# Softmax reciprocals of a fused attention kernel: from VectorE's reciprocal to a power of minus one on GpSimd

## The chip, the cores and the metric

The kernel runs on one core of a Trainium2 chip. The metric is its time on the device in microseconds, as the median of several executions. Engines: TensorE (PE: matmuls and transposes; PEld is its weight load), VectorE (DVE), ScalarE (ACT), GpSimd (POOL), and SyncE (SP), which issues the DMAs here. TensorE's granted clock was at its upper level (2.4 GHz) in nearly the whole profile, 0.996 of it in the mean.

## The reference

Two layers over x of shape (2, 1024, 256), in float32:

```python
# layer 0
nx = layer_norm(x);  q = nx @ Wq;  k, v = ctx @ Wk, ctx @ Wv        # ctx: (2, 154, 256)
evidence = softmax(q k^T / 16) @ v
combined = concat([nx, evidence, anchor])
probs = softmax(combined @ router_W + router_b)                     # 3 experts
h = silu(combined @ e_w1 + e_b1);  routed = sum_e probs_e * (h_e @ e_w2 + e_b2)
g = sigmoid(silu(combined @ gate_w1 + gate_b1) @ gate_w2 + gate_b2)
x = x + g * (routed @ out_w + out_b)
# layer 1: 16 heads of 16
xq, xkv = ada_ln(x, cond), ada_ln(ctx, cond)
out = concat_heads(softmax(q_h k_h^T / 4) @ v_h)
x = x + out @ Wp + bp
```

The change concerns the softmax of layer 1: the product with v is made with the exponentials as they are, and the result is multiplied by one over their sum.

## The kernel before

The 2048 tokens are worked in eight tiles of 256 (t = 0 to 7; `LAST` is 7, `NEXT` 6). A planner written out by hand (`PLAN`, `PLAN_OF`, `SETUP`) gives each step (a name, a tile and an index) a time slot; `DELAY` shifts it for single engines; and `order(engine)` sorts an engine's steps by that time. So five in-order instruction queues are fixed when the program is built, and semaphores with a name for each step tie them together. While the hidden units of tile t run (seven units; steps `za`, `z`, `h`, `p`: hidden matmuls, tanh on ScalarE, product on VectorE, a split into a high half on ScalarE and a low half `hidden_low` on GpSimd at L1620, second matmul `p`, which reads both halves), the attention of layer 1 of tile t - 1 and t - 2 and the layer 0 attention of tile t + 1 are laid between them.

In layer 1 the steps of a tile are: `stack` (SyncE copies the queries into the stacked layout of head pairs, four groups), `most` (16 score matmuls with the maximum of each taken on VectorE, L1463, in a ring of three banks of PSUM), `row` (the maxima, transposed and copied back), `score` (12 matmuls and exponentials), `value` (matmuls into `value_bank`; its value operand has columns of ones, so that the sums of the exponentials come out as rows of the same result, four rows in each group of 32), `raw` (ScalarE copies the bank to SBUF in two halves, L1142), `sum` on GpSimd, `sums`, `dup`, `out` on VectorE, `out` on ScalarE, `outl` and `proj`.

`sum` adds the four 128x256 slices of the copied result (L1666, L1671, L1673), which leaves in one 128x256 tile the sums of all 16 heads, each in a row of its own. `sums` on VectorE takes the reciprocal in place (L1477):

```python
v.reciprocal(total[:, :], total[:, :]).then_inc(vector_sums, 1)
```

`dup` (L1486) shuffles the outputs so that each stands twice in its group of 32 rows, `out` spreads the reciprocals over the rows with one shuffle for each group (L1496) and multiplies (L1498), ScalarE's `out` rounds the product to its high half, and `outl` (L1506) makes the low half, which `proj` needs. The last tile is worked in two halves with tiles of their own (`last_sums_first`, `last_sums`), and its `sums`, `dup` and `out` come twice.

GpSimd has one in-order queue. In a steady tile its steps around `sum` are: the second pair of adds (L1671, L1673), `probs` of the tile after (two products, L1643 and L1644, whose transposes TensorE does at L1889), `hidden_low` of unit 4 (L1620). It takes rstd of three layer norms as a power of minus one half, in a 128x2 instruction (L1534).

Of the kernel before, what the change touches and what calls it, by code (L numbers as in the profile page):

```python
# [13 lines left out]
ALU = mybir.AluOpType  # L14
# [3 lines left out]
P = 128  # L18
# [71 lines left out]
def packed(np, v):  # L90
# [17 lines left out]
    for b in range(BATCH):  # L108
# [114 lines left out]
        "dup": ["d"],  # L223
        "sums": ["r"],
        "out": ["o"],
# [25 lines left out]
    "tensor": {  # L251
        "norm": 1.4, "qx": 0.31, "prob": 1.4, "keyx": 0.3, "qx_last": 0.2,
    },
    "scalar": {
        "cv": -4.9, "ck": 0.3, "fold": 0.1, "vw": 0.54, "vt": 0.3, "w2": 0.6, "keyx": 0.6, "norm": 1.9, "att": 0.7,
        "logit": 1.7, "z": 0.81, "h": 0.3, "gate": 0.4, "qx": 0.4, "query": 0.1, "row": -0.4, "score": 0.2,
        "out": 1.6, "xhat_last": -0.7, "qx_last": 0.2, "query_last": 0.2, "row_last": 0.5, "score_last": 0,
        "raw_last": 0.1, "out_last": 1.54,
    },
# [3 lines left out]
        "res_last": -1.5, "qn_last": -1.3, "shift_last": -1.1, "qlow_last": 1, "query_last": 1.1, "most_last": 1.5,  # L263
        "row_last": 1.2, "proj_last": -10.8, "dup_last": 0.7, "sums_last": -1.6, "out_last": 1.4, "outl_last": 1.4,
    },
    "gpsimd": {
        "h": 0.6, "ln": 0.86, "qn": -0.2, "low": 0.9, "keyn": 1.2, "split": 2.1,
    },
# [11 lines left out]
PLAN = {  # L280
    "dup": (37.2, 49.2), "za": -0.4, "step": 1.99, "z": 0.38, "h": 1.5, "p": 3.3, "again": -6.4, "vw": -38.8,
    "ln": 0.2, "norm": 1.6, "low": 6.6, "att": 7.9, "prob": 9.1, "route": 12.3, "logit": 14.4, "res": 17.4,
    "qn": 18.4, "shift": 18.5, "xhat": 19.3, "qx": 19.54, "qlow": 20.1, "query": 20.7,
    "most": (22.11, 22.29, 23.89, 24.92, 26.01, 26.34, 27.35, 28.05), "row": (29.2, 30.6),
    "stack": (15.3, 16.8, 20.9, 23.1),
    "score": (32, 32.1, 32.1, 32.7, 33.5, 33.7, 34.2, 34.3, 34.3, 35.4, 35.5, 35.6),
    "value": (33.88, 34.18, 35.92, 36.25), "raw": (35.5, 36.9), "sum": (35.3, 36.4), "sums": (38.1, 47.7),
    "out": (38.34, 56.69), "outl": (43.37, 97.85), "proj": 43.6, "last": (16, 59.3), "reload": 45.3, "init": 5.2,
}

PLAN_OF = {
    0: {
        "most": (21.92, 23.13, 24.17, 24.59, 25.33, 27.11, 27.44, 28.14), "qlow": 19.3, "query": 19.9, "qn": 17.5,
        "h": 1.3, "qx": 18.7, "xhat": 18.2,
    },
    1: {
        "logit": 15.4, "z": 0.62,
    },
# [6 lines left out]
    6: {  # L305
        "init": 6.5, "score": (30.5, 30.6, 30.6, 31.3, 31.4, 31.6, 31.9, 31.9, 31.9, 32.5, 32.6, 33),
        "raw": (34.4, 34.5), "proj": 47.7, "most": (21.9, 22, 24.8, 25.8, 26.5, 27.3, 27.4, 28), "ln": 0.9,
        "value": (31.83, 31.84, 34.15, 34.75), "norm": 1.79, "stack": (16.3, 16.7, 21.5, 21.9),
    },
    7: {  # L310
        "route": 13.2, "most": (19.2, 19.2, 19.3, 19.4, 19.4, 19.6, 20.3, 20.5), "init": 5.6, "sums": (28.4, 36),
        "za": -0.73, "score": (22.06, 22.59, 22.73, 23.07, 23.16, 23.16, 23.63, 23.73, 24.03, 24.23, 24.34, 24.54),
        "outl": (33.4, 33.8), "row": (19.96, 21.53), "h": 1.2, "p": 3.5, "last": (39.5, 39.7), "query": 18.06,
        "xhat": 17.7, "ln": 0.5, "value": (23.2, 23.5, 24.7, 25.8), "proj": 38, "logit": 14.9, "out": (27.3, 33.2),
        "raw": (23.1, 28.7), "qlow": 18, "qx": 17.62, "dup": (24.9, 28.7), "step": 1.96,
    },
}
SETUP = {
    "vw": (1.6, 3, 3.8, 4.5, 6.1, 7.7, 8.2), "vt": (0.8, 2, 2.9, 3.9, 7.1, 9.1, 10.7),
    "unit": (0.99, 2.23, 3.75, 4.08, 9.23, 9.4, 9.94), "w2": (7.4, 10.3, 11.1, 13, 14.2, 17.9), "norm": -0.3,  # L320
    "low": 1.7, "att": 2, "prob": 2.8, "route": 3.8, "logit": 4.75, "cb": 4.3, "bq": 12.2, "split": (8.74, 13.12),
    "keyn": (11.4, 12.5), "keyx": (12.4, 13.8), "key": (13.4, 17.8), "mod": (9.2, 9.6, 10.3, 10.6), "ck": 10.8,
    "fold": (0.6, 12), "late": (6.6, 14.9), "ln": -6.8, "silu": -0, "group": 1.1, "gsplit": 5.6, "setup2": -12,
    "bias1": -7.9,
    "fill": (120.23, 120.27, 120.77, 120.82, 121.09, 121.76, 121.98, 127.05, 127.63, 128.86, 129.54, 129.71, 131.45, 131.47),
    "sel": 114.7, "unstack": 105, "bias2": (26.4, 26.7), "zero": 102.7,
}
# [7 lines left out]
def schedule():  # L335
# [37 lines left out]
    for t in range(NT):  # L373
# [30 lines left out]
        for h in range(parts_of(t)):  # L404
            for name in ("row", "dup", "sums", "out", "outl"):
                place(at + plan(t, name)[h], (name, t, h))
# [40 lines left out]
def build(nc, a, out):  # L447

    with ExitStack() as ctx:
# [199 lines left out]
        def step_sem(engine, stage):  # L649
# [111 lines left out]
        def sums_of(t, h):  # L761
            return (SUMF, SUML)[h] if t == LAST else SUM
# [396 lines left out]
        def _(dve):  # L1159
# [355 lines left out]
            def proj(key):  # L1515
# [6 lines left out]
                     "att": att, "prob": prob, "route": route, "logit": logit, "z": hidden, "init": init, "evac": evac,  # L1522
                     "res": res, "qn": qn, "shift": shift, "qlow": qlow, "query": query, "most": most, "row": row, "dup": dup, "outl": outs_low, "sums": sums,
                     "out": outs, "proj": proj, "last": last_add}
# [5 lines left out]
        def _(pool):  # L1530
# [128 lines left out]
            def sums(key):  # L1659

                t, h = key[1:]
                pool.wait_ge(scalar_raw, upto(scalar_raw, ("raw", t, h), "v"))
                if h == 0:
                    if 0 < t < LAST:
                        pool.wait_ge(vector_out, upto(vector_out, ("out", t - 1, 0), "o"))
                    nc.gpsimd.tensor_tensor(sums_of(t, 0)[:, :], raw_of(t)[:, 0, :], raw_of(t)[:, 1, :], ALU.add).then_inc(gpsimd_sum, 1)  # L1666
                elif t == LAST:
                    nc.gpsimd.tensor_tensor(SUML[:, :], RAWL[:, 2, :], RAWL[:, 3, :], ALU.add).then_inc(gpsimd_sum, 1)
                else:
                    pool.wait_ge(gpsimd_sum, upto(gpsimd_sum, ("sum", t, 0), "s"))  # L1670
# [483 lines left out]
```

## Time and profile before

| | us |
|---|---|
| median of three timed runs | 438.0 (437.63 to 439.25) |
| the profiled execution's own time | 439.08 |
| its span, first to last instruction | 436.9 |
| TensorE busy | 422.1 (97%) |
| VectorE busy | 296.3 (68%) |
| ScalarE busy | 223.6 (51%) |
| GpSimd busy | 175.0 (40%) |
| one steady tile (from a step of one to the same of the next) | 43.3 |

Busy is the time in which an engine has an instruction under way; it says nothing of whether anyone waits for it. Overlapping matmuls are counted once. A time such as "290.60" is microseconds from the span's start. In a timeline the number behind the start is the duration of all instructions merged in the row, whose count stands at the end as x2, x4.

### The profile page before, as it was taken

To read this page: it belongs to the slowest core of one execution; us is meant where nothing else is said; L and a number is where in the kernel's file an instruction comes from. 1 tells how busy PE (TensorE), PEld (TensorE's weight loads), DVE (VectorE), ACT (ScalarE), POOL (GpSimd) and SP (SyncE) were. 2 spreads that over 40 slices of the span, in tenths; PEclk is the share of its full clock that TensorE was granted. 3 is DMA by queue.
4 is the path that set the end of the run, shared out by engine and by line. 5 is a ranking of instruction groups with operands and counts; after the bars stand their busy time and mean duration, and the time that the engine had idled before them with its cause. 6 is when DMAs were issued, how large, how long until landed. Compare 5 with 4: busy or idle time off the path is not lost.

```text
span 436.9 us, 9623 instructions
## 1 busy us (share of the span) xinstructions
PE 422.1 (97%) x3629; PEld 384.7 (88%) x3629; DVE 296.3 (68%) x748; ACT 223.6 (51%) x487; POOL 175.0 (40%) x184
## 2 busy tenths in 40 slices
PE   7899999999999999999999999999999899979996
PEld 6578999989998899889998899889988898868876
DVE  2785566674675696739863797389658755891797
ACT  2868643255347543764367246724672356326271
POOL 4545474553353526324523344344433632330020
PEclk9999999999999999999999999999999999998999
DMA  8786102531100210023000300030003021300301
GB/s 288 252 298 269 50 2 47 142 91 31 44 5 1 63 59 30 24 78 116 2 5 13 109 1 5 14 86 0 5 20 80 0 56 28 80 3 26 72 3 48
DMA packets 16837, 27.80 MB, mean 64 GB/s; under 512 B 3800, under 2 KB 9112, under 8 KB 16664
## 3 DMA queue, kind: packets, MB, share of 16 engines
q1 hardware_dynamic: 16664, 27.19, 21.2%
q8 instruction: 29, 0.48, 0.5%
q14 instruction: 16, 0.13, 0.1%
q10 hardware_dynamic: 128, 0.01, 0.0%
HBM read 15.94 MB, written 2.10 MB: 41 GB/s over the span
## 4 chain that ended last, share of the span: by engine, by line
PE 77%; DVE 15%; issue 3%; ACT 3%; DMA 1%; SPq 1%; ACTq 0%
PE hidden_banks L1688 7%; PE hidden_banks L1690 7%; PE hidden_banks L1689 7%; PE score_banks L1695 6%; PE score_banks L2060 5%; PE token_bank L1688 5%; PE token_bank L1689 5%; PE token_bank L1690 5%; PE score_banks L2030 4%; PE value_bank L2083 3%; PE value_bank L2086 3%; PE value_bank L1695 3%; DVE head_maxima L1463 3%; PE hidden_banks L1913 2%; DVE sums L1477 2%
## 5 line engine op out<-in xcount | busy, mean ns | idle before, releaser
L1620 POOL TENSOR_TENSOR hidden_low<-hidden,hidden_high 128x512 fp32r<-128x512 f32 x56 | 72.8, 1300 | 123.5 <-ACT hidden_high L1072 123.4
L1463 DVE TENSOR_REDUCE head_maxima<-score_banks 128x2 f32<-128x308 f32 x128 | 54.6, 473 | 17.1 <-PE score_banks L2030 15.0
L1688 PE MATMUL hidden_banks<-normed_high,hidden_w_high 128*128 128x256 f32 x224 | 64.2, 287 | 0.8 <-issue 0.8
L1689 PE MATMUL hidden_banks<-normed_high,hidden_w_low 128*128 128x256 f32 x224 | 62.5, 279 | 0.0
L1690 PE MATMUL hidden_banks<-normed_low,hidden_w_high 128*128 128x256 f32 x224 | 62.5, 279 | 0.0
L1132 ACT ACTIVATE exp_ring<-score_banks 128x512 f32<-128x512 f32 x96 | 52.6, 600 | 18.8 <-PE score_banks L2060 17.5
L1072 ACT CAST hidden_high<-hidden 128x512 fp32r<-128x512 f32 x56 | 34.8, 622 | 48.2 <-DVE hidden L1380 48.1
L1688 PE MATMUL token_bank<-expert_out_high,hidden_high 128*128 128x256 f32 x192 | 55.7, 290 | 0.0
L1064 ACT ACTIVATE hidden<-hidden_banks 128x512 f32<-128x512 f32 x56 | 33.3, 595 | 41.6 <-PE hidden_banks L1913 40.0
L1690 PE MATMUL token_bank<-expert_out_low,hidden_high 128*128 128x256 f32 x192 | 53.4, 278 | 0.0
L1689 PE MATMUL token_bank<-expert_out_high,hidden_low 128*128 128x256 f32 x192 | 53.4, 278 | 0.0
L1380 DVE SCALAR_TENSOR_TENSOR hidden<-hidden,hidden_banks 128x512 f32<-128x512 f32 x56 | 38.2, 683 | 18.5 <-ACT hidden L1064 18.3
L1688 PEld LDWEIGHTS hidden_banks<-normed_high,hidden_w_high 128*128 128x128 f32 x224 | 42.1, 188 | 2.1 <-issue 2.0
L1689 PEld LDWEIGHTS hidden_banks<-normed_high,hidden_w_low 128*128 128x128 f32 x224 | 42.3, 189 | 0.1
L1690 PEld LDWEIGHTS hidden_banks<-normed_low,hidden_w_high 128*128 128x128 f32 x224 | 42.0, 188 | 0.0
L1688 PEld LDWEIGHTS token_bank<-expert_out_high,hidden_high 128*128 128x128 f32 x192 | 36.2, 188 | 0.5 <-issue 0.2
L1689 PEld LDWEIGHTS token_bank<-expert_out_high,hidden_low 128*128 128x128 f32 x192 | 36.3, 189 | 0.2
L1690 PEld LDWEIGHTS token_bank<-expert_out_low,hidden_high 128*128 128x128 f32 x192 | 36.1, 188 | 0.0
L2030 PE MATMUL score_banks<-pair_keys,query_stack 96*128 96x308 f32 x112 | 29.4, 335 | 2.5 <-DVE head_maxima L1463 1.4
L1913 PE MATMUL hidden_banks<-probs_T_tail,context_w_tail 100*128 100x256 f32 x112 | 31.6, 282 | 0.0
L1689 PE MATMUL hidden_banks<-probs_T_high,context_w_low 128*128 128x256 f32 x112 | 31.2, 279 | 0.0
L1688 PE MATMUL hidden_banks<-probs_T_high,context_w_high 128*128 128x256 f32 x112 | 31.2, 279 | 0.0
(294 smaller groups left out, 1111.5 us busy)
## 6 DMA issues: line engine op xcount, KB each, us to landing
unit_weights<-units SPq DMA_DIRECT2D x7, 768.0 KB, 6.0
query_stack<-queries_high SPq DMA_DIRECT2D x56, 64.0 KB, 2.0
tokens<-x SPq DMA_DIRECT2D x8, 256.0 KB, 3.7
query_stack<-queries_low SPq DMA_DIRECT2D x28, 64.0 KB, 2.0
w_slice<-units SPq DMA_DIRECT2D x7, 256.0 KB, 3.0
out<-tokens SPq DMA_DIRECT2D x7, 256.0 KB, 2.4
w_T<-folds SPq DMA_DIRECT2D x6, 256.0 KB, 6.1
pair_keys<-keys_high SPq DMA_DIRECT2D x16, 77.0 KB
```

Of the source, the lines that this page charges most:

```text
L1064: nc.scalar.activation(TB[:, ring(t, u), :], Z[:, hidden_bank(t, u), :], ACT.Tanh, scale=0.5).then_inc(scalar_z, 1)
L1072: nc.scalar.copy(SH[:, ring(t, u), :], TB[:, ring(t, u), :]).then_inc(scalar_h, 1)
L1132: nc.scalar.activation(E[:, w % ERING, :], S[:, ring_of[key][0], :], ACT.Exp).then_inc(scalar_score, 1)
L1380: v.scalar_tensor_tensor(out=TB[:, ring(t, u), :], in0=TB[:, ring(t, u), :], scalar=1.0, in1=Z[:, hidden_bank(t, u), :], op0=ALU.add, op1= ...
L1463: v.tensor_reduce(MX[:, s, first:first + step + 1:step], S[:, ring_of[key][0], 0:2 * CTX].rearrange("p (j n) -> p j n", j=2), AX.X, ALU.ma ...
L1620: nc.gpsimd.tensor_tensor(SL[:, ring(t, u), :], TB[:, ring(t, u), :], raw(SH[:, ring(t, u), :]), ALU.subtract).then_inc(gpsimd_h, 1)
L1688: mm(out_, lh, rh, start=start, stop=False, skip_group_check=skip)
L1689: mm(out_, ll, rh, start=False, stop=False, skip_group_check=skip)
L1690: return mm(out_, lh, rl, start=False, stop=stop, skip_group_check=skip)
L1695: last = mm(out_, l, r, start=(i == 0), stop=(i == len(pairs) - 1))
L1913: return mm(half, VWD[0:BROWS, b, c], PTD[0:BROWS, t % 2, :], start=False, stop=True)
L2030: mm(bank, QS[0:STACK, c, P * s:P * s + P], KS[b][0:STACK, c, :, :].rearrange("p j n -> p (j n)"), start=True, stop=True).then_inc(tensor_ ...
```

## The change

The step `sums` is gone from VectorE. GpSimd's `sum` gets a third (or, for the last tile, second) instruction: the power of minus one of the whole 128x256 tile, with an exponent tile of 128x1 broadcast along the row, behind a wait for its own last add. VectorE's `out` waits for GpSimd's `sum` now. The planner's numbers change as well, and with them the order on each engine: on SyncE the store of a finished tile moves ahead of the second group of `stack`, and the reloads of weights in the middle of the kernel (`again`) one place ahead; on VectorE `init` moves behind `qlow`, and in tile 5 `dup` behind `z` of unit 4; on ScalarE `score` 11 moves ahead of the `h` of unit 3 in tiles 2 to 6, and the last tile's `out` of the first half ahead of its second `raw`; on TensorE `prob` of tile 2 moves behind three steps; and a few steps of the setup trade places.

```diff
+        MINUS = put("minus_one", [P, 1])
...
+                v.memset(MINUS[:, :], -1.0)
...
-            def sums(key):
-                t, h = key[1:]
-                total = sums_of(t, h)
-                dve.wait_ge(gpsimd_sum, upto(gpsimd_sum, ("sum", t, 1 if t < LAST else h), "s"))
-                v.reciprocal(total[:, :], total[:, :]).then_inc(vector_sums, 1)
...
             def outs(key):
...
-                dve.wait_ge(vector_sums, upto(vector_sums, key, "r"))
+                dve.wait_ge(gpsimd_sum, upto(gpsimd_sum, ("sum", t, 1 if t < LAST else h), "s"))
...
                 pool.wait_ge(scalar_raw, upto(scalar_raw, ("raw", t, h), "v"))
...
+                total, outs = sums_of(t, h), raw_of(t)
+                add = lambda left, right: nc.gpsimd.tensor_tensor(total[:, :], left, right, ALU.add)
+                if t < LAST and h == 0:
+                    if t:
                         pool.wait_ge(vector_out, upto(vector_out, ("out", t - 1, 0), "o"))
+                    add(outs[:, 0, :], outs[:, 1, :]).then_inc(gpsimd_sum, 1)
+                    return
+                if t == LAST:
+                    add(outs[:, 2 * h, :], outs[:, 2 * h + 1, :]).then_inc(gpsimd_part, 1)
                 else:
                     pool.wait_ge(gpsimd_sum, upto(gpsimd_sum, ("sum", t, 0), "s"))
+                    add(total[:, :], outs[:, 2, :]).then_inc(gpsimd_part, 1)
+                    pool.wait_ge(gpsimd_part, 2 * t + 1)
+                    add(total[:, :], outs[:, 3, :]).then_inc(gpsimd_part, 1)
+                pool.wait_ge(gpsimd_part, 2 * t + 2 if t < LAST else 2 * t + 1 + h)
+
+                nc.gpsimd.tensor_tensor(total[:, :], total[:, :], MINUS[:, :].to_broadcast([P, TILE]), ALU.pow).then_inc(gpsimd_sum, 1)
```

Of the planner's numbers, those that move steps named above:

```diff
-        "row_last": 1.2, "proj_last": -10.8, "dup_last": 0.7, "sums_last": -1.6, "out_last": 1.4, "outl_last": 1.4,
+        "row_last": 1.2, "proj_last": -10.8, "dup_last": 0.7, "sums_last": -1.6, "out_last": 1.4, "outl_last": 1.8,
-        "query": 13.4, "row": -3.6, "proj": 1.5, "last": -2.1, "key": -0.9, "place": 11.3, "query_last": 3.7,
+        "query": 13.4, "row": -3.6, "proj": 1.3, "last": -2.1, "key": -0.9, "place": 11.3, "query_last": 3.7,
-    "stack": (15.3, 16.8, 20.9, 23.1),
+    "stack": (15.5, 17, 21.1, 23.3), "score": (32, 32.1, 32.1, 32.7, 33.5, 33.7, 34.2, 34.3, 34.3, 35.4, 35.5, 35.6),
-    "out": (38.34, 56.69), "outl": (43.37, 97.85), "proj": 43.6, "last": (16, 59.3), "reload": 45.3, "init": 5.2,
+    "out": (38.4, 56.7), "outl": (43.38, 97.79), "proj": 43.7, "last": (16, 59.3), "reload": 45.4, "init": 6.1,
```

## Rows read from the trace of the kernel before

**Rows 1.** The page: span, and busy time of each engine.

```profile
span 436.9 us, 9623 instructions
PE 422.1 (97%) x3629; PEld 384.7 (88%) x3629; DVE 296.3 (68%) x748; ACT 223.6 (51%) x487; POOL 175.0 (40%) x184
```

**Rows 2.** TensorE's waits: us in total, times, the longest.

```profile
PE score_banks L2030 <- DVE head_maxima L1463: 1.4, 6, 0.3
...
PE hidden_banks L2094 <- DVE last_outs_low L1506: 0.9, 1, 0.9
```

**Rows 3.** The chain that ended last, from 415 us: start, us, what.

```profile
427.91 1.72 DVE last_sums L1477
...
429.66 0.81 DVE last_sums_spread L1496 x3
...
431.90 0.39 PE hidden_banks L2094
```

**Rows 4.** VectorE's groups by form: count, busy us, mean ns, idle before.

```profile
L1380 DVE SCALAR_TENSOR_TENSOR hidden<-hidden,hidden_banks 128x512 f32<-128x512 f32 x56 | 38.2, 683 | 18.5 <-ACT hidden L1064 18.3
...
L1477 DVE RECIPROCAL sums<-sums 128x256 f32<-128x256 f32 x7 | 12.3, 1753 | 0.0
```

**Rows 5.** Timeline of VectorE in a steady tile.

```profile
289.64 1.77 DVE L1477 RECIPROCAL sums<-sums 128x256 f32<-128x256 f32 x1
291.30 0.83 DVE L1463 TENSOR_REDUCE head_maxima<-score_banks 128x2 f32<-128x308 f32 x2
...
292.02 0.47 DVE L1496 STREAM_SHUFFLE sums_spread<-sums 128x256 f32<-128x256 f32 x1
```

**Rows 6.** Timeline of TensorE, the same tile, and tile 5's.

```profile
290.60 0.44 PE L2030 MATMUL score_banks<-pair_keys,query_stack 96*128 96x308 f32 x2
...
292.07 0.27 PE L1889 MATMUL head_bank<-constants,probs 128*128 128x128 f32 x1
...
292.79 0.28 PE L1688 MATMUL token_bank<-expert_out_high,hidden_high 128*128 128x256 f32 x1
...
295.84 0.41 PE L2030 MATMUL score_banks<-pair_keys,query_stack 96*128 96x308 f32 x1 [0.22 <-DVE head_maxima L1463]
...
380.30 0.28 PE L1688 MATMUL token_bank<-expert_out_high,hidden_high 128*128 128x256 f32 x1
```

**Rows 7.** GpSimd's groups by form.

```profile
L1620 POOL TENSOR_TENSOR hidden_low<-hidden,hidden_high 128x512 fp32r<-128x512 f32 x56 | 72.8, 1300 | 123.5 <-ACT hidden_high L1072 123.4
L1631 POOL TENSOR_SCALAR x_hat<-tokens,mean_var,rstd 128x256 f32<-128x256 f32 x16 | 21.4, 1344 | 0.8
...
L1673 POOL TENSOR_TENSOR sums<-sums,outs_and_sums 128x256 f32<-128x256 f32 x7 | 5.2, 740 | 0.5
```

**Rows 8.** The line of rstd alone: ns min/median/max, first and last start.

```profile
L1534 POOL TENSOR_TENSOR rstd<-mean_var,minus_half x18: 690/713/1671, 9.5 to 393.7; 128x2 f32<-128x2 f32 x18
```

**Rows 9.** Timeline of GpSimd, the same tile, and tile 5's last add pair.

```profile
288.15 0.75 POOL L1673 TENSOR_TENSOR sums<-sums,outs_and_sums 128x256 f32<-128x256 f32 x1
288.85 0.61 POOL L1643 TENSOR_TENSOR probs<-exps,softmax_small 128x256 f32<-128x256 f32 x1
289.42 0.45 POOL L1644 TENSOR_TENSOR probs<-exps,softmax_small 128x156 f32<-128x156 f32 x1
290.48 1.29 POOL L1620 TENSOR_TENSOR hidden_low<-hidden,hidden_high 128x512 fp32r<-128x512 f32 x1 [0.61 <-ACT hidden_high L1072]
...
375.17 0.74 POOL L1673 TENSOR_TENSOR sums<-sums,outs_and_sums 128x256 f32<-128x256 f32 x1
```

**Rows 10.** Timeline of the last tile's sums: GpSimd, and ScalarE's copy.

```profile
421.15 1.52 POOL L1666 TENSOR_TENSOR last_sums_first<-last_outs_and_sums 128x256 f32<-128x256 f32 x1 [3.97 <-ACT last_outs_and_sums L1142]
427.01 0.82 POOL L1668 TENSOR_TENSOR last_sums<-last_outs_and_sums 128x256 f32<-128x256 f32 x1 [4.33 <-ACT last_outs_and_sums L1142]
...
426.34 0.59 ACT L1142 COPY last_outs_and_sums<-value_bank 128x512 f32<-128x512 f32 x1 [0.74 <-PE value_bank L2086]
```

**Rows 11.** SyncE's queue in the same tile, the last copy of group 1.

```profile
284.77 0.59 SPq L870 DMA_DIRECT2D query_stack<-queries_high  x1
```

More of the change, by code:

```diff
@@ L223 @@
         "dup": ["d"],
-        "sums": ["r"],
         "out": ["o"],
@@ L251 @@
     "tensor": {
-        "norm": 1.4, "qx": 0.31, "prob": 1.4, "keyx": 0.3, "qx_last": 0.2,
+        "norm": 1.4, "qx": 0.3, "prob": 1.4, "keyx": 0.3, "qx_last": 0.2,
     },
     "scalar": {
-        "cv": -4.9, "ck": 0.3, "fold": 0.1, "vw": 0.54, "vt": 0.3, "w2": 0.6, "keyx": 0.6, "norm": 1.9, "att": 0.7,
-        "logit": 1.7, "z": 0.81, "h": 0.3, "gate": 0.4, "qx": 0.4, "query": 0.1, "row": -0.4, "score": 0.2,
+        "cv": -4.9, "ck": 0.3, "fold": 0.1, "vw": 0.5, "vt": 0.3, "w2": 0.6, "keyx": 0.6, "norm": 1.9, "att": 0.7,
+        "logit": 1.7, "z": 0.8, "h": 0.3, "gate": 0.4, "qx": 0.4, "query": 0.1, "row": -0.4, "score": 0.2,
         "out": 1.6, "xhat_last": -0.7, "qx_last": 0.2, "query_last": 0.2, "row_last": 0.5, "score_last": 0,
-        "raw_last": 0.1, "out_last": 1.54,
+        "raw_last": 0.1, "out_last": 1.4,
     },
@@ L280 @@
 PLAN = {
-    "dup": (37.2, 49.2), "za": -0.4, "step": 1.99, "z": 0.38, "h": 1.5, "p": 3.3, "again": -6.4, "vw": -38.8,
-    "ln": 0.2, "norm": 1.6, "low": 6.6, "att": 7.9, "prob": 9.1, "route": 12.3, "logit": 14.4, "res": 17.4,
+    "dup": (37.3, 49.2), "za": -0.4, "step": 1.99, "z": 0.38, "h": 1.6, "p": 3.3, "again": -8.2, "vw": -39.4,
+    "ln": 0.2, "norm": 1.6, "low": 6.7, "att": 7.9, "prob": 9.2, "route": 12.3, "logit": 14.4, "res": 17.4,
     "qn": 18.4, "shift": 18.5, "xhat": 19.3, "qx": 19.54, "qlow": 20.1, "query": 20.7,
-    "most": (22.11, 22.29, 23.89, 24.92, 26.01, 26.34, 27.35, 28.05), "row": (29.2, 30.6),
-    "stack": (15.3, 16.8, 20.9, 23.1),
-    "score": (32, 32.1, 32.1, 32.7, 33.5, 33.7, 34.2, 34.3, 34.3, 35.4, 35.5, 35.6),
-    "value": (33.88, 34.18, 35.92, 36.25), "raw": (35.5, 36.9), "sum": (35.3, 36.4), "sums": (38.1, 47.7),
-    "out": (38.34, 56.69), "outl": (43.37, 97.85), "proj": 43.6, "last": (16, 59.3), "reload": 45.3, "init": 5.2,
+    "most": (22.11, 22.29, 23.89, 24.92, 26.01, 26.34, 27.35, 28.05), "row": (29.1, 30.6),
+    "stack": (15.5, 17, 21.1, 23.3), "score": (32, 32.1, 32.1, 32.7, 33.5, 33.7, 34.2, 34.3, 34.3, 35.4, 35.5, 35.6),
+    "value": (33.89, 34.19, 35.95, 36.26), "raw": (35.5, 36.9), "sum": (35.5, 36.4), "sums": (38.1, 47.7),
+    "out": (38.4, 56.7), "outl": (43.38, 97.79), "proj": 43.7, "last": (16, 59.3), "reload": 45.4, "init": 6.1,
 }
@@ L292 @@
     0: {
-        "most": (21.92, 23.13, 24.17, 24.59, 25.33, 27.11, 27.44, 28.14), "qlow": 19.3, "query": 19.9, "qn": 17.5,
-        "h": 1.3, "qx": 18.7, "xhat": 18.2,
+        "query": 19.9, "qx": 18.7, "qn": 17.5, "most": (21.92, 23.13, 24.17, 24.59, 25.33, 27.11, 27.44, 28.14),
+        "qlow": 19.3, "xhat": 18.2, "h": 1.3,
     },
     1: {
-        "logit": 15.4, "z": 0.62,
+        "logit": 15.4, "z": 0.6,
     },
@@ L305 @@
     6: {
-        "init": 6.5, "score": (30.5, 30.6, 30.6, 31.3, 31.4, 31.6, 31.9, 31.9, 31.9, 32.5, 32.6, 33),
-        "raw": (34.4, 34.5), "proj": 47.7, "most": (21.9, 22, 24.8, 25.8, 26.5, 27.3, 27.4, 28), "ln": 0.9,
-        "value": (31.83, 31.84, 34.15, 34.75), "norm": 1.79, "stack": (16.3, 16.7, 21.5, 21.9),
-    },
-    7: {
[L311 to L315, printed above, removed]
+        "ln": 0.9, "proj": 47.7, "value": (31.83, 31.84, 34.15, 34.75),
+        "most": (21.9, 22, 24.8, 25.8, 26.5, 27.3, 27.4, 28), "raw": (34.4, 34.5), "norm": 1.79,
+        "score": (30.5, 30.6, 30.6, 31.3, 31.4, 31.6, 31.9, 31.9, 31.9, 32.5, 32.6, 33),
+        "stack": (16.3, 16.7, 21.5, 21.9),
+    },
+    7: {
+        "score": (22.1, 22.6, 22.7, 23.1, 23.2, 23.2, 23.6, 23.7, 24, 24.2, 24.3, 24.5), "h": 1.2,
+        "last": (39.5, 39.8), "most": (19.2, 19.2, 19.3, 19.4, 19.4, 19.6, 20.3, 20.3), "proj": 37.9,
+        "value": (23.25, 23.55, 24.75, 25.85), "ln": 0.5, "qlow": 18, "query": 18.06, "p": 3.5, "step": 1.96,
+        "route": 13.2, "qx": 17.62, "out": (27.4, 33.2), "dup": (24.9, 28.7), "raw": (23.15, 28.75),
+        "outl": (33.5, 33.9), "za": -0.73, "row": (19.96, 21.53), "xhat": 17.7,
     },
@@ L404, in schedule @@
         for h in range(parts_of(t)):
-            for name in ("row", "dup", "sums", "out", "outl"):
+            for name in ("row", "dup", "out", "outl"):
                 place(at + plan(t, name)[h], (name, t, h))
@@ L1522, in _ @@
                      "att": att, "prob": prob, "route": route, "logit": logit, "z": hidden, "init": init, "evac": evac,
-                     "res": res, "qn": qn, "shift": shift, "qlow": qlow, "query": query, "most": most, "row": row, "dup": dup, "outl": outs_low, "sums": sums,
+                     "res": res, "qn": qn, "shift": shift, "qlow": qlow, "query": query, "most": most, "row": row, "dup": dup, "outl": outs_low,
                      "out": outs, "proj": proj, "last": last_add}
```

23 lines of the change are left out of this document (7 added, 16 removed).

## The prediction

> **What bounds the kernel now.** I read first the head of the page, for the busy shares: TensorE is busy for 422 us of a span of 436.9 us, VectorE for 296, GpSimd for 175 [rows 1]. Work taken off VectorE is worth something only where TensorE, or the end, waits for VectorE. So the second view is the list of TensorE's waits: it waited six times, 1.4 us in all, for VectorE's reductions of the scores (`head_maxima`), and once, 0.90 us, for the low half of the last attention outputs [rows 2]. The third is the chain that ended last, from 416 us on: there it is VectorE's alone, with the reciprocals of L1477 in it, up to the matmul at 431.90 [rows 3]. So there are two regimes: up to 416 us a full TensorE with holes of a quarter of a microsecond, then a VectorE chain. The change has to be costed in each.
>
> **What is removed.** Nine reciprocals of 128x256: seven of 1753 ns on `sums` and two on the last tile's halves, the second of them in the chain at 427.91; that is 9 x 1.75 = 15.8 us of VectorE [rows 3, 4]. Almost all of it lies beside TensorE's work.
>
> Steady tiles (0 to 4, one each 43.3 us; the stretch from 281 to 298 us stands for them). The reciprocal at 289.64 is followed by two reductions at 291.30, the four spreading shuffles from 292.02, and in the end the reduction for which TensorE waited 0.22 us before 295.84 [rows 5, 6]. The two reductions can't come before their matmuls at 290.60 plus 0.44, so VectorE moves forward by only about 0.6 us (the reductions end at 291.5 and the shuffles start there, not at 292.06). That covers the hole of 0.22 us. The holes that stand behind a reciprocal are four of the six; at some 0.21 us each they give 0.84 us. The whole 1.4 us of rows 2 is the bound above, nothing the bound below. In tile 5 VectorE's order has hidden(7, 4) ahead of `dup` now, which takes back about 1.2 of the 1.75 us there; what is left still covers a hole of 0.2 us.
>
> **What is added.** Nine `pow` instructions of 128x256 on GpSimd, behind the last add of each sum, and a wait between them; call the time of one T. The trace has no such instruction. The nearest rows bound it from both sides. Below: an add of 128x256 takes 740 ns and a subtraction of 128x512 1300 ns, so 2.2 ns a column and 180 ns once [rows 7]; with a broadcast operand, as the new instruction has one, the shape takes 0.62 us at 288.85 [rows 9], and that is the floor. Above: a `pow` of 128x2 takes 713 ns in the median of 18 [rows 8]. If its 533 ns above the fixed 180 belonged to its two columns, a column would cost 267 ns and T would be 68 us. If they are paid once per instruction, and the columns then stream as in the other rows, T = 0.71 + 254 x 2.2 ns = 1.27 us, or with the 4.6 ns a column of the two-operation `x_hat` row (1344 ns less 180, over 256), 1.9 us. I take 1.5 us, in this last pair: by shape the new instruction is like the 128x256 rows, all of which lie between 0.6 and 1.4 us, and only by operation like the row of two columns, which mostly shows what starting costs. This is a choice and not a reading, and it carries most of the risk.
>
> What T delays in a steady tile: the last add starts at 288.15 and ends at 288.9; `pow` follows, so the reciprocals are there at 288.95 + T. Behind it in GpSimd's queue stand the next tile's `probs` (two products at 288.85 and 289.42, done at 289.87, 1.0 us) and `hidden_low`, which now starts at 290.48 and takes 1.29 us [rows 9]. `hidden_low` is read by the matmuls at 292.79, `probs` by the transposes at 292.07 [rows 6]. So `hidden_low` has to start by 291.45, which holds as long as 288.95 + T + 1.0 is below it: **T up to 1.5 us is covered, and each microsecond above it is one of TensorE's, in five tiles**. `probs` is late only from T = 2.1, and VectorE's shuffles only from T = 2.5 (291.5 less 288.95). In tile 5 the add starts at 375.17 and the reader is at 380.30; no `probs` lies between, and T up to 3.0 is covered [rows 6, 9].
>
> The tail: the first half's sum of the last tile and tile 6's come early enough. For the last, the raw outputs are copied at 426.34, the add starts at 427.01 and takes 0.82 us [rows 10]; the reciprocal ran from 427.91, and the shuffles began at 429.66 [rows 3]. With `pow` they begin at 427.87 + T + 0.05. That is **1.75 - T earlier: 0.25 us at T = 1.5**, and from the shuffles on nothing changes. ScalarE has the cast of the first half's outputs ahead of the copy at 426.34 now. That cast needs the first half's add (from 421.15, 0.8 us, or the 1.52 us of the row, where VectorE's product ran at the same time), `pow`, 1.5 us of VectorE's shuffles and product, and 0.6 us itself. So it is done at 424.2 + T to 424.9 + T, and delays the copy only from a T between 1.4 and 2.1 [rows 10].
>
> A rule speaks against this kind of move. The trace first: the same kind of subtraction or product over 128x512 takes 1300 ns on GpSimd and 683 ns on VectorE, 1.9 times [rows 4, 7]. The Trainium skill (GPSIMD Engine Reference, section on performance versus the Vector engine) calls VectorE about twice as fast for ordinary elementwise work and advises against moving it; this trace's 1.9 agrees. Applied to the reciprocal it would be a rival of its own, priced below from the rows.
>
> **The reordered steps.** The planner's numbers move, too. SyncE stores the finished tile ahead of the second group of `query_stack` copies instead of behind it; this shifts those copies, the last of which is issued at 284.77, by the 0.6 us of one issue and by what the store occupies; their reader is the reduction's matmul at 290.60 [rows 6, 11], so some 3 us of cover remain. `init` goes behind `qlow`, the exponential of score 11 ahead of a hidden cast, one `prob` of TensorE behind three steps of matmuls, and some steps of the setup change places. All of them lie under a TensorE that is 97% busy, and I cost them at nothing; if the covers are gone, each is worth one such instruction, 0.6 us a tile at most. What an engine issues stays the same otherwise.
>
> **The sum.** 0.84 us from the steady tiles and 0.25 us from the tail, 1.1 us. The profiled execution took 439.08 us with a span of 436.9, so it would come to 438.0; the median of the three timed runs is 438.0, and the same difference gives **436.9 us**. A difference of 0.5%, 2.2 us, is about what can be told from no change here.
>
> **The rivals.**
> (a) `pow` runs at nearly the speed of an add, T = 0.74, and the new order closes a further microsecond of the small waits. Tail 1.0, steady 0.84 to 1.4, order up to 1: 2.9 to 3.3 us less, about 435. For it speaks that most of the 713 ns may be start-up; against it, that the reordered steps have nearly no hole to close.
> (b) The other side: moved work costs on GpSimd twice what it costs on VectorE, T = 3.3 (1.75 x 1.9). Then `hidden_low` ends at 294.56 instead of 292.79, 1.8 us of TensorE in each of five tiles, 0.3 us in tile 5. In the tail the cast holds up the copy by 1.2 us and `pow` is 1.55 us longer than the reciprocal. 9.1 + 0.3 + 2.7 - 0.8 = 11.3 us more: 449. The mechanism is one wait, TensorE's for `hidden_low` behind `pow` in GpSimd's queue, and it decides from T = 1.5, which is just where I put T. That makes it the strongest rival.
> (c) Each column costs what the two-column row says, T = 68 us. Then 5 x 66.9 us in the steady tiles, 65 in tile 5, and three such instructions in a row in the tail, some 197 us: about 1,030 us. Only the two-column row speaks for it, but it is the one row of this operation.
> (d) All is hidden: the holes of TensorE stay, because it meets the next limit (its own issue) at once, and T = 1.75 gives nothing in the tail: 438. Its difference from the forecast is too small to be told by the time.
>
> **How the numbers follow.** Forecast with T from 1.2 to 1.9, and (d) with it: 0.42, its own range 436.1 (T = 0.74: 1.85 us less) to 439. Case (a) 0.24. Case (b) and all T between 2.2 and 5 with it 0.22. Case (c) 0.12. Faster by over 0.5%: (a), 0.24. Within 0.5%: 0.42. Slower by over 0.5%: (b) and (c), 0.34. The range starts at 434.5, below (a), and ends at 455, above (b) with room for T = 4; left out are (c) and the tails of (a) and (b), 0.2 together.
>
> **What would show it.** The new group on GpSimd, `pow` of 128x256: its mean is T. `hidden_low` behind it should start at about 291.5 by this tile's clock, and TensorE's list of waits should have no entry for it; the entry for `head_maxima` should fall from 1.4 to about 0.6 us. VectorE's busy time should be down by 15.8 us, GpSimd's up by 9 T. The chain of the tail should have GpSimd in it at the last sum, followed by the shuffles. The prediction is wrong if T is above 2 us (then TensorE waits for `hidden_low`, once a tile), or if the reordered steps bring waits for DMA that the trace of before hasn't.

## The result

The changed kernel takes 801.1 us in the median of four runs (800.3 to 802.0), against 438.6 us for the kernel before (437.6 to 442.6). The ratio of the times is 1.825, with a 95% interval of 1.820 to 1.831. The forecast was 436.9, with a range from 434.5 to 455.0. It was wrong by a factor of 1.8. Of its rivals, (c), a cost for every column, is the right mechanism.

The page of the changed kernel, the lines that answer to [rows 1], the granted clock by fortieths of the span, and what moved in the list of groups:

```profile
span 798.5 us, 9624 instructions
PE 440.3 (55%) x3629; PEld 403.5 (51%) x3629; DVE 287.2 (36%) x740; ACT 223.6 (28%) x487; POOL 543.8 (68%) x193
PEclk9999999955997589855995599658985799555555
L1673 POOL TENSOR_TENSOR sums<-sums,minus_one 128x256 f32<-128x256 f32 x7 | 288.0, 41139 | 0.6
```

VectorE lost 9 us of busy time, where 15.8 was forecast: the nine reciprocals are gone, but two casts in the setup took 2.6 us more, and the steady tiles' products with the spread sums (L1492) another 2.6, with a median of 1.75 us instead of 1.23. No run here isolates the cause of either. GpSimd gained 369. One power of minus one of 128x256 takes **41.14 us**; with the two of the last tile there are nine, 370 us. TensorE's clock falls to its lower level in each stall.

TensorE's waits after, where [rows 2] had 1.4 us in six waits and one of 0.9 us:

```profile
PE head_bank L1889 <- POOL probs L1638: 193.5, 6, 38.8
PE head_bank L2094 <- DVE next_outs_low L1500: 74.2, 1, 74.2
PE hidden_banks L2094 <- DVE last_outs_low L1500: 40.1, 1, 40.1
PE token_bank L1688 <- POOL hidden_low L1614: 37.9, 1, 37.9
```

The first row is the steady tiles: five waits of some 38.6 us (the sixth is the 0.5 us in the setup that was there before). The fourth is tile 5, the second and third are the tail. Together 345.7 us less the 0.5, and less the 0.9 us that the third already had before, make 344.3 us of new waiting. TensorE's busy time rose by 18.2 us with the same 3629 matmuls, so that 362.5 us are accounted for; the span grew by 361.6, and the small holes that closed are the rest.

A steady tile, in GpSimd's timeline:

```profile
151.94 1.55 POOL L1658 TENSOR_TENSOR sums<-sums,outs_and_sums 128x256 f32<-128x256 f32 x2 [1.72 <-ACT outs_and_sums L1141]
153.57 41.14 POOL L1673 TENSOR_TENSOR sums<-sums,minus_one 128x256 f32<-128x256 f32 x1
194.69 0.61 POOL L1637 TENSOR_TENSOR probs<-exps,softmax_small 128x256 f32<-128x256 f32 x1
195.26 0.45 POOL L1638 TENSOR_TENSOR probs<-exps,softmax_small 128x156 f32<-128x156 f32 x1
195.66 1.27 POOL L1614 TENSOR_TENSOR hidden_low<-hidden,hidden_high 128x512 fp32r<-128x512 f32 x1
```

This is the stretch of [rows 9] with one instruction more. TensorE in the same stretch, behind the stall and six microseconds later:

```profile
195.76 0.47 PE L1889 MATMUL head_bank<-constants,probs 128*128 128x128 f32 x1 [38.77 <-POOL probs L1638]
...
197.86 0.41 PE L1688 MATMUL token_bank<-expert_out_high,hidden_high 128*128 128x256 f32 x1
198.07 0.41 PE L1689 MATMUL token_bank<-expert_out_high,hidden_low 128*128 128x256 f32 x1
...
202.17 0.28 PE L1688 MATMUL hidden_banks<-normed_high,hidden_w_high 128*128 128x256 f32 x1
202.29 0.28 PE L1689 MATMUL hidden_banks<-normed_high,hidden_w_low 128*128 128x256 f32 x1
```

The matmuls start 0.21 us apart at first and 0.12 us apart from 202 us on. The windows of the same stretch have the granted clock in the sixth place behind the times (us, busy of PE, PEld, DVE, ACT, POOL, then the clock):

```profile
153.60:194.80 41.20, 3.39 (x29) 3.18 (x27) 1.69 (x6) 1.22 (x2) 41.20 (x2) 0.59 0.04 11
194.80:200.00 5.20, 4.24 (x20) 4.18 (x21) 4.55 (x11) 1.35 (x2) 2.79 (x4) 0.50 0.01 2
200.00:205.00 5.00, 5.00 (x36) 5.00 (x36) 3.55 (x9) 1.34 (x4) 0.62 (x1) 0.82 0.00 0
205.00:210.00 5.00, 5.00 (x41) 4.78 (x40) 4.43 (x11) 0.63 (x2) 3.57 (x3) 1.00 0.02 3
```

TensorE stood still for 38.8 us, worked behind it at half of its clock (the lower level, 1.2 GHz) for some 6 us, and then at full clock again. The chain of the tail has the last three powers in series, with what lies between them:

```profile
661.72 41.14 POOL sums L1673
702.86 0.71 POOL last_sums_first L1658
703.63 41.14 POOL last_sums_first L1673
744.80 0.79 DVE last_sums_spread L1490 x3
745.61 0.70 DVE last_outs_twice L1492
746.36 0.50 issue
746.86 0.59 ACT last_outs_and_sums L1141
747.52 0.73 POOL last_sums L1658
748.29 41.17 POOLq L448
789.50 0.79 DVE last_sums_spread L1490 x3
```

Here the moved cast on ScalarE shows: the copy of the last outputs at 746.86 comes behind the shuffles and the product that need the second power, so the third can't start before. The prediction had named this delay, for a T above 1.4 to 2.1 us.

### The profile page after: what moved, and what is told of

Same layout as the page of the kernel before. It is cut to its first block, busy times and chain, and to the rows that moved or that the text cites. A ratio compares the mean times of both kernels' runs of the same rounds, so it can differ in the third digit from the quotient of the medians.

```text
span 798.5 us, 9624 instructions
## 1 busy us (share of the span) xinstructions
PE 440.3 (55%) x3629; PEld 403.5 (51%) x3629; DVE 287.2 (36%) x740; ACT 223.6 (28%) x487; POOL 543.8 (68%) x193
## 4 chain that ended last, share of the span: by engine, by line
PE 45%; issue 31%; POOL 13%; POOLq 5%; DVE 2%; ACT 2%; DMA 1%; SPq 0%; ACTq 0%
POOL sums L1673 5%; POOLq L448 5%; POOL last_sums_first L1673 5%; PE hidden_banks L1688 4%; PE hidden_banks L1689 4%; PE hidden_banks L1690 4%; PE score_banks L1695 4%; PE token_bank L1688 3%; PE token_bank L1690 3%; PE token_bank L1689 3%; PE score_banks L2060 3%; PE score_banks L2030 2%; PE value_bank L2083 2%; PE value_bank L2086 1%; PE value_bank L1695 1%
## 5 line engine op out<-in xcount | busy, mean ns | idle before, releaser
L1673 POOL TENSOR_TENSOR sums<-sums,minus_one 128x256 f32<-128x256 f32 x7 | 288.0, 41139 | 0.6
L1889 PE MATMUL head_bank<-constants,probs 128*128 128x128 f32 x16 | 6.0, 386 | 193.5 <-POOL probs L1638 193.5
L1889 PEld LDWEIGHTS head_bank<-constants,probs 128*128 128x128 f32 x16 | 2.9, 181 | 195.1 <-POOL probs L1638 195.1
L1688 PE MATMUL token_bank<-expert_out_high,hidden_high 128*128 128x256 f32 x192 | 58.8, 306 | 37.9 <-POOL hidden_low L1614 37.9
L1688 PEld LDWEIGHTS token_bank<-expert_out_high,hidden_high 128*128 128x128 f32 x192 | 38.7, 202 | 38.5 <-issue 38.1
L1690 PE MATMUL token_bank<-expert_out_low,hidden_high 128*128 128x256 f32 x192 | 56.4, 294 | 0.0
L1689 PE MATMUL token_bank<-expert_out_high,hidden_low 128*128 128x256 f32 x192 | 56.3, 293 | 0.0
L2094 PE MATMUL head_bank<-proj_w_high,next_outs_low 128*128 128x256 f32 x8 | 3.5, 434 | 74.2 <-DVE next_outs_low L1500 74.2
L1673 POOL TENSOR_TENSOR last_sums<-last_sums,minus_one 128x256 f32<-128x256 f32 x1 | 41.1, 41127 | 0.1
```

The source lines that it names most:

```text
L1673: nc.gpsimd.tensor_tensor(total[:, :], total[:, :], MINUS[:, :].to_broadcast([P, TILE]), ALU.pow).then_inc(gpsimd_sum, 1)
L1688: mm(out_, lh, rh, start=start, stop=False, skip_group_check=skip)
L1689: mm(out_, ll, rh, start=False, stop=False, skip_group_check=skip)
L1690: return mm(out_, lh, rl, start=False, stop=stop, skip_group_check=skip)
```

## The experiments

Eleven kernels. They ask three things: what sets the duration of a power (first three below), what the queue does with a given duration T (next six), and whether anything else in the change costs time (last two).

**How long a power takes, by columns.**

```diff
+                n = (4, 8, 16, 32, 64, 128, 192, 8, 16)[t + (h if t == LAST else 0)]
-                nc.gpsimd.tensor_tensor(total[:, :], total[:, :], MINUS[:, :].to_broadcast([P, TILE]), ALU.pow).then_inc(gpsimd_sum, 1)
+                nc.gpsimd.tensor_tensor(total[:, 0:n], total[:, 0:n], MINUS[:, :].to_broadcast([P, n]), ALU.pow).then_inc(gpsimd_sum, 1)
```

> The changed kernel with the power on only the first n columns of the sums, n by tile 4, 8, 16, 32, 64, 128, 192 and on the last tile's halves 8 and 16 (the other columns stay sums, so the output is wrong there). Theory, fixed part and a cost per column from the rows of 2 columns (0.713 us) and 256 (41.14 us): 0.159 us a column and 0.395 us once, so 1.03, 1.67, 2.9, 5.5, 10.6, 20.8 and 30.9 us. Rival, that small shapes have a rate of their own and a larger one goes to a slower path: 2.2 to 10 ns a column at first (below 1.5 us at n = 32), then a step.

GpSimd's groups by form (busy us, mean ns):

```profile
L1674 POOL TENSOR_TENSOR sums<-sums,minus_one 128x192 f32<-128x192 f32 x1 | 30.9, 30939 | 0.1
L1674 POOL TENSOR_TENSOR sums<-sums,minus_one 128x128 f32<-128x128 f32 x1 | 20.7, 20740 | 0.1
L1674 POOL TENSOR_TENSOR sums<-sums,minus_one 128x64 f32<-128x64 f32 x1 | 10.5, 10533 | 0.1
...
L1674 POOL TENSOR_TENSOR sums<-sums,minus_one 128x32 f32<-128x32 f32 x1 | 5.4, 5427 | 0.1
...
L1674 POOL TENSOR_TENSOR sums<-sums,minus_one 128x16 f32<-128x16 f32 x1 | 2.9, 2907 | 0.1
...
L1674 POOL TENSOR_TENSOR sums<-sums,minus_one 128x8 f32<-128x8 f32 x1 | 1.6, 1648 | 0.1
...
L1674 POOL TENSOR_TENSOR sums<-sums,minus_one 128x4 f32<-128x4 f32 x1 | 1.0, 1019 | 0.1
```

A straight line over the whole range: (30939 - 1648) / 184 = 159 ns a column, and 0.4 us once. There is no faster path for small shapes and no step. The first theory holds to 2%, the rival is out.

**The same, by what the numbers are.** Powers of 32 columns on other bases and exponents.

```diff
+                base = (total[:, 0:n], ONES[:, 0:n], ONES[:, 0:n], ONES[:, 0:n], total[:, 0:n], total[:, 0:n], CN[:, C_ID:C_ID + n], total[:, 0:n], total[:, 0:n])[t + (h if t == LAST else 0)]
+                power = (MINUS, MINUS, HALF, TWO, TWO, ZERO, TWO, MINUS, MINUS)[t + (h if t == LAST else 0)]
+                nc.gpsimd.tensor_tensor(total[:, 0:n], base, power[:, 0:1].to_broadcast([P, n]), ALU.pow).then_inc(gpsimd_sum, 1)
```

> The changed kernel with powers of 32 columns on other operands, by tile: 0 sums to -1, 1 ones to -1, 2 ones to -0.5, 3 ones to 2, 4 sums to 2, 5 sums to 0, 6 a unit matrix to 2, the last tile's halves sums to -1 (the rest is left as sums, so the output is wrong). Theory, that the cost is the general power routine's whatever the numbers: all 5.49 us within 2%. Rival, that it depends on the operands (negative bases in the rows that hold outputs, or the exponent): ones to -1 or the power of 2 clearly shorter, 2 us or below.

```profile
L1682 POOL TENSOR_TENSOR sums<-sums,minus_one 128x32 f32<-128x32 f32 x1 | 5.4, 5427 | 0.1
...
L1682 POOL TENSOR_TENSOR sums<-ones,two 128x32 f32<-128x32 f32 x1 | 5.4, 5425 | 0.1
L1682 POOL TENSOR_TENSOR sums<-sums,zero_power 128x32 f32<-128x32 f32 x1 | 5.4, 5425 | 0.1
L1682 POOL TENSOR_TENSOR sums<-ones,minus_one 128x32 f32<-128x32 f32 x1 | 5.4, 5424 | 0.1
```

All nine lie between 5424 and 5427 ns. Exponents of 2, 0, -0.5 and -1 cost the same, and so do bases of one, of a unit matrix and of the sums.

**The same, by partitions.** Powers of 32 columns on 128, 64, 32, 16 partitions and 1, and of 1, 128 and 8 columns.

```diff
+                rows, n = ((128, 32), (64, 32), (32, 32), (16, 32), (1, 32), (128, 1), (16, 128), (128, 8), (128, 8))[t + (h if t == LAST else 0)]
+                nc.gpsimd.tensor_tensor(total[0:rows, 0:n], total[0:rows, 0:n], MINUS[0:rows, :].to_broadcast([rows, n]), ALU.pow).then_inc(gpsimd_sum, 1)
```

> The changed kernel with powers on fewer partitions, by tile, partitions x columns: 128x32, 64x32, 32x32, 16x32, 1x32, 128x1, 16x128, the last tile's halves 128x8 (the rest is left as sums, so the output is wrong). Theory, that a column costs the same however many partitions are in it: 5.49 us for the first five, 0.55 for 128x1, 20.8 for 16x128. Rival, that the routine works through a core's partitions one after the other, so that a column of one partition costs a sixteenth of one of sixteen: 1x32 at about 0.7 us, the others of 32 columns at 5.5.

```profile
L1674 POOL TENSOR_TENSOR sums<-sums,minus_one 16x128 f32<-16x128 f32 x1 | 20.7, 20725 | 0.1
...
L1674 POOL TENSOR_TENSOR sums<-sums,minus_one 128x32 f32<-128x32 f32 x1 | 5.4, 5425 | 0.1
...
L1674 POOL TENSOR_TENSOR sums<-sums,minus_one 1x32 f32<-1x32 f32 x1 | 5.4, 5415 | 0.1
...
L1674 POOL TENSOR_TENSOR sums<-sums,minus_one 128x1 f32<-128x1 f32 x1 | 0.6, 561 | 0.1
```

A column costs the same with one partition in it as with 128. The rival is out. By the program only 16 of the 128 rows of the tile hold sums, so with the 4096 sums in 32 full columns a power would take 5.4 us, still three times the reciprocal of 256 columns on VectorE.

**No reciprocal at all.** GpSimd's part as before the change, nothing in the place of the reciprocal.

```diff
-                nc.gpsimd.tensor_tensor(total[:, :], total[:, :], MINUS[:, :].to_broadcast([P, TILE]), ALU.pow).then_inc(gpsimd_sum, 1)
```

> The changed kernel without the power, and with no reciprocal anywhere: the outputs are multiplied by the sums, not divided. It shows the most that any faster reciprocal could give. The prediction's sum at T = 0: 0.84 us of TensorE's holes and 1.75 us of the tail, 2.6 us less than before, 436.0. Rival 1, that TensorE's holes stay: 1.75 us less, 436.9. Rival 2, that VectorE's 15.8 us free much more than the holes show, through earlier releases of banks: 433 or below.

437.6 us, 0.9991 of the time before (0.9973 to 1.0010): 1.1 us in the medians, and not separable from none in the ratio; 436.0 was expected, and 436.9 by the first rival. A part of the 1.1 us is the clock: among the runs with a mean granted clock of 1.000 the medians are 437.2 (five runs) and 437.9 (twelve of the kernel before). The profiled span is 435.5 against 436.9. So the most that this change could have given, with an operation that costs nothing, is some 0.3%.

**One product in the place of the power.**

```diff
-                nc.gpsimd.tensor_tensor(total[:, :], total[:, :], MINUS[:, :].to_broadcast([P, TILE]), ALU.pow).then_inc(gpsimd_sum, 1)
+                nc.gpsimd.tensor_tensor(total[:, :], total[:, :], MINUS[:, :].to_broadcast([P, TILE]), ALU.mult).then_inc(gpsimd_sum, 1)
```

> The changed kernel with a product by minus one in the place of the power of minus one (same shape, same operands, same waits; the reciprocal is left out and the sign is wrong). T is 0.6 to 0.8 us. By the prediction's steps: 0.84 + 1.75 - 0.75, 1.8 us less than before, 436.8, no TensorE wait for hidden_low. Rival, that the added wait and the longer GpSimd queue already cost TensorE something: 438.6 or more, and an entry for hidden_low or probs in TensorE's waits.

437.55 us, 0.9980 (0.9970 to 0.9991), a gain of 0.2%, with each product at 0.61 us and T at 0.7; at a granted clock of 1.000 it is 437.5 (nine runs) against 437.9. TensorE's waits have no `hidden_low`, and those for `head_maxima` fell from 1.4 to 0.6 us:

```profile
PE score_banks L2030 <- DVE head_maxima L1463: 0.6, 2, 0.3
```

These waits are as forecast. The tail is not: this kernel and the one without any reciprocal end at the same span of 435.5, although the last sums are ready 0.6 us earlier in the latter. VectorE's timeline at the end of each, first without a reciprocal:

```profile
427.62 0.45 DVE L1490 STREAM_SHUFFLE last_sums_spread<-last_sums 128x256 f32<-128x256 f32 x1
...
432.49 0.90 DVE L1506 TENSOR_TENSOR tokens<-tokens,hidden_banks 128x256 f32<-128x256 f32 x2 [0.97 <-PE hidden_banks L2093]
```

and with one product:

```profile
428.23 0.45 DVE L1490 STREAM_SHUFFLE last_sums_spread<-last_sums 128x256 f32<-128x256 f32 x1
...
432.46 0.90 DVE L1506 TENSOR_TENSOR tokens<-tokens,hidden_banks 128x256 f32<-128x256 f32 x2 [0.67 <-PE hidden_banks L2095]
```

The shuffles start 0.6 us apart, the last additions at the same time. TensorE sets the time there. It has the 18 matmuls of tile 6's projection to do first, and in both kernels it goes on from them to those of the last tile without a pause, at 430.62 and 430.60 us. Before the change it waited 0.90 us between the two [rows 2], about 1.1 us from start to start. That is the most that the tail could give, whatever becomes earlier on VectorE.

**Two products, and four.** In-place products in a row, each behind a wait for the one before it. The edit for four:

```diff
+                for k in range(4):
+                    last = nc.gpsimd.tensor_tensor(total[:, :], total[:, :], MINUS[:, :].to_broadcast([P, TILE]), ALU.mult)
+                    if k < 3:
+                        last.then_inc(chained, 1)
+                        pool.wait_ge(chained, 3 * (t + (h if t == LAST else 0)) + k + 1)
+                last.then_inc(gpsimd_sum, 1)
```

> As the one before with two products by minus one in a row, each behind a wait for the one before it (no reciprocal, which is left out), so T is about 1.5 us, the value that the prediction chose. By its steps TensorE is just covered: 0.84 + 0.25, 1.1 us less than before, 437.5. Rival, that TensorE waits earlier than at T = 1.5: above 439.

> The changed kernel with four products by minus one in a row in the place of the power (no reciprocal, which is left out), T about 3.1 us. By the prediction's steps each microsecond above 1.5 costs TensorE one in each of five tiles: 5 x 1.6 = 8 us, 0.1 in tile 5, in the tail 1.4 from the longer chain and 1.0 from the cast that holds up the copy, less 0.84: about 9.7 us more than before, 448. Rival, that only probs is read early and hidden_low has more room (threshold 2.1 us): 5 us in place of 8, 445. Rival, that the queue has slack in other places and takes it up: below 442.

Two products (1.30 us, T of 1.4): 439.9 us, 1.0032 (1.0011 to 1.0054). By the time alone this is the rival, which said above 439. By the trace it is not: TensorE's list has no wait for GpSimd other than the 0.5 us of the setup, and in GpSimd's timeline four of the five steady tiles last as long as with one product, to 0.02 us. So the cover holds. The twelve runs lie between 437.3 and 442.2 us, and in the main they follow the clock: a span of 435.4 with a mean granted clock of 1.000, 438.0 with 0.992, and 440.4 with 0.988. In the profiled run the clock was 0.83 from 10 to 20 us and 0.94 from 372 to 400 us; the second stretch is the same in the profile of the kernel before. Of the two runs at 1.000 one took 437.3 us, near the expected 437.5, and the other 438.6. Why this kernel met the lower clock more often than the one with one product stays open.

Four products (2.70 us, T of 2.8): 447.9 us, 1.021 (1.018 to 1.024), close to the expected 448, but the total hides two errors. TensorE's waits from 140 to 400 us:

```profile
PE token_bank L1694 <- POOL hidden_low L1615: 1.5, 4, 0.4
PE head_bank L1895 <- POOL probs L1639: 1.3, 4, 0.3
```

Both readers are late now, in four tiles of five. The recorded waits, 2.8 us in all, are less than the delay: in each stall TensorE's last matmul still counts as busy for its full 0.28 us, although the next would have started after 0.12. The delay itself is in the starts of GpSimd's first product. From tile 0 to tile 5 they go from 153.70 to 382.11 us, 4.3 us more than with one product (153.25 to 377.34), at full clock in both: some 1.05 us in each of four tiles and 0.1 in the other. 5 x (2.8 - 1.5) gives 6.5. From there to the end it takes 6.0 us more than with one product: TensorE waits 3.1 us for the last outputs, and from 400 us on its granted clock is 0.92 instead of 1.00. The forecast had nothing for the clock.

**The power in one tile.** A power in tile 2, a product in all others.

```diff
+                power = ALU.pow if t == 2 else ALU.mult
+                nc.gpsimd.tensor_tensor(total[:, :], total[:, :], MINUS[:, :].to_broadcast([P, TILE]), power).then_inc(gpsimd_sum, 1)
```

> The power in tile 2 only, a product by minus one in all others (the reciprocal is left out there). Theory A, the wait alone: 41.14 us less the 0.61 of a product and less the cover that is left behind a product, 1.5 us: 39.0 us more than with one product, 476.6. Theory B, the wait and the clock: after the stall TensorE's matmuls stand 213 ns apart instead of 118 for some 6 us, which costs another 2.7 us, so 479.3. Rival C, that some of a single stall is made up later, by steps that are ahead after it: below 474.

479.9 us (479.1 to 480.5, four runs), 42.4 us more than with one product in another job, and TensorE's wait is this:

```profile
PE head_bank L1890 <- POOL probs L1638: 39.2, 2, 38.8
```

The wait is 38.8 us of it; the theory with the clock gave 479.3, the one without 476.6. In the profiled run 1.4 us of the difference lie ahead of the power, where the granted clock was 0.83 from 10 to 20 us and 0.96 from 60 to 104. From there on, by the starts of GpSimd's first product in tiles 0 and 5 (154.64 and 420.04 us), the power costs 41.3 us, where the theory with the clock had 41.7 and the one without 39.0. Nothing is made up later. The cover is 41.14 + 0.08 - 38.8, 2.4 us by the recorded wait, for `probs`, which is read first.

**The power in the tail alone.** In tiles 6 and 7, with products in tiles 0 to 5 (the same edit with `t >= NEXT`).

> The power in tiles 6 and 7 only (three instructions), a product by minus one in tiles 0 to 5 (the reciprocal is left out there). In the profile of the changed kernel the first of the three starts at 661.7 and the last ends at 789.5, 127.7 us; with one product in their place the same stretch took 11.2 us. So 116.6 us more than with one product, 554, and up to 2 us more where TensorE's last matmuls run at the lower clock: 554 to 556. Rival, that they overlap work which VectorE and ScalarE do in between, or that more than the three instructions is in series: off by over 10 us.

557.3 us (two runs), where 554 to 556 were expected: 1.3 us above the range, and far from the rival's 10. The profiled run has a granted clock of 0.91 in its first 20 us and is 1.1 us behind the one with one product before the first power. The tail's three powers cost some 120 us by themselves, and the other six the remaining 244.

**The order alone.** The kernel before with the changed planner's numbers; the two `sums` steps of the last tile keep their slots.

```diff
     7: {
+        "sums": (28.4, 36),
```

> The kernel before with the changed planner's numbers, so with all the reordered steps, and the reciprocals still on VectorE (computes the reference). The theory, that the 362 us come from the 41.1 us of each power of minus one and from nothing else: the order changes at most 1 us either way, 437.6 to 439.6 against 438.6. The rival, that the reordered steps bring waits for DMA or put SyncE's store in the way of the query copies: 0.6 us a tile or more, 443 and above, with a new entry for query_stack among TensorE's waits.

439.8 us, 1.0033 (1.0017 to 1.0049): a small loss, 0.2 us above the range that was expected. Its one new wait in the profile is in tile 5, where `dup` stands behind `hidden(7, 4)` and the reciprocal is still in VectorE's queue:

```profile
383.29 0.41 PE L2031 MATMUL score_banks<-pair_keys,query_stack 96*128 96x308 f32 x1 [1.43 <-DVE head_maxima L1464]
```

The wait there was 0.2 us before. Waits for `query_stack` didn't grow, so the store ahead of the copies costs nothing that shows.

**The power with the old order.** The changed steps with the planner's numbers of before.

> The changed kernel with the planner's numbers of before, so without the reordered steps (computes the reference). Theory, that the power's duration is the whole cause: 801 us within 5. Rival, that the reordered steps make the stall longer, by work that could have run under the power: 780 or below.

797.2 us in two runs, 1.818 (1.809 to 1.827). The order is worth some 4 us in 360, and 3.3 of them are the moved cast: TensorE's wait for `last_outs_low` is 36.8 us instead of 40.1, because the chain of the tail has the third power right behind the second:

```profile
744.33 0.70 POOL last_sums L1658
745.07 41.17 POOLq L448
```

No run here has another way to a reciprocal, such as a divide or a power with a constant exponent on GpSimd, or either of them on VectorE.

## Why the prediction was wrong

**The step that failed is the value of T.** The prediction bounded it by 0.62 us and 68 us and took 1.5, "by shape the new instruction is like the 128x256 rows ... and only by operation like the row of two columns, which mostly shows what starting costs". The row of two columns [rows 8] in fact holds both: 0.41 us once and 0.153 us for each of its columns, by the instructions of one, two and four columns (561, 713 and 1019 ns). The measured T is 41.14 us. The prediction had read 533 ns above what an add pays at the start, and the whole of it went to the fixed part for no reason but the shape; 306 of it belonged to the two columns. The two readings of that one row were 50 times apart, and the trace of before has all its 18 powers at the same shape, so it couldn't tell them apart. Both rivals on the slow side rested on rows as well. (b) took the 1.9 times of a subtraction or product over to the reciprocal, and here the power takes 23 times as long as VectorE's reciprocal. (c), which took the row of the same operation at its word, was given 0.12. It said 1,030 us with 267 ns a column. With the measured T its steps give 5 x 39.6 + 38.1, and its three powers in a row 116.6 by the traces (127.7 us from the first start to the last end, where one product has 11.2): 353 us more than before. The other 10 of the 363 us are, as far as the traces show, the lower clock behind the stalls.

**The mechanism behind it held.** GpSimd's queue is where it hurts, `probs` and `hidden_low` stand behind the power, and TensorE waits once a tile. The size of the cover was nearly right: 1.5 us was forecast. With four products, T = 2.8, four of the five tiles are 1.05 us longer, so their cover is some 1.75 us; the fifth covers nearly all of the 2.8. Above the cover each microsecond of T was one of TensorE's wait, in five tiles, as forecast.

**The steady gain showed in the waits and not in the time.** TensorE's waits for `head_maxima` fell from 1.4 to 0.6 us with one product, as the prediction had it. But the five tiles are no shorter. The windows from GpSimd's last add in tile 0 to the one in tile 5 before the change, and between the products that follow it with one product, columns as above:

```profile
151.20:375.20 224.00, 221.21 (x1959) 204.42 (x1958) 160.03 (x390) 116.86 (x250) 90.56 (x85) 1.00 0.14 39
153.20:377.30 224.10, 222.73 (x1958) 207.45 (x1957) 150.37 (x383) 116.78 (x251) 93.22 (x89) 1.00 0.14 38
```

TensorE's idle time there fell from 2.8 to 1.4 us, its busy time rose by as much with the same work, and the stretch takes 223.95 us before (151.22 to 375.17) and 224.09 after, at full clock in both. That is what rival (d) had said of this part; what took up the time isn't shown. Rival (a) shared the error, and its own terms add up to 1.8 to 3.4 us, not 2.9 to 3.3.

**The gain of the tail was oversized.** "1.75 - T earlier ... and from the shuffles on nothing changes" left out TensorE, whose matmuls for tile 6 become the next limit. The prediction had the number, the wait of 0.90 us in [rows 2], and used it only to show who waits. With T = 0 or T = 0.7 the gain of both parts together is 1.1 us in the medians, and 0.7 or 0.4 at a granted clock of 1.000, not 2.6 or 1.9. The kernel with one product is also 1.2 us later than the one before when the steady tiles begin (its last add of tile 0 starts at 152.43 us, against 151.22).

**The reordered steps** were costed at nothing and cost 1.1 us in the medians when the reciprocals stay on VectorE, and some 4 us when the power takes 41. The part of it that shows is the step that the prediction named, `dup` behind `hidden(7, 4)`; it had called the hole there covered, because the reciprocal would be gone.

**The clock** doesn't appear in the prediction's sums. A stall of TensorE costs more than itself: 41.3 us for a wait of 38.8.

## What to carry to other kernels

When an operation is known from one small shape only, its duration there must not be split into a fixed part and a part per column by analogy with other operations; price both readings, and if they differ by more than the gain at stake, measure two sizes before moving anything. Before pricing the gain, find how long the next engine on the chain waits: a step that ends 1.75 us earlier is worth no more than the 1 us or so for which its reader stood still. A hole that closes is not yet time gained: compare the same stretch before and after. And where a wait of TensorE is added, look at the granted clock behind it; here each stall of 38.8 us cost another 2 to 3.

## What the runs showed of the hardware

GpSimd's power takes 0.40 us and 0.159 us a column, on 1 to 192 and 256 columns, with one partition or 128, and with any of the exponents tried. A product of the same shape takes 0.61 us, where the power takes 41.14, 67 times as long. VectorE's reciprocal takes 1.75 us for 256 columns; in that time the power does 8 (1648 ns).

The scatter of the kernels near 438 us goes in the main with the clock: twelve runs of the kernel with two products go from a span of 435.4 us at a mean granted clock of 1.000 to 440.4 us at 0.988, about 4 us for each hundredth. The kernel with one product, in the same job, kept between 0.992 and 1.000 and scattered over 1.1 us.
